# Deformable-convolution stage: one PSUM bank for the projection, three for the transposes, rows duplicated by DMA, positions on VectorE

## What is computed

```
yp = iy + ky + offset[..., 0]          # 8 groups, 9 taps
xp = ix + kx + offset[..., 1]
val = bilinear sample of coarse_up at (yp, xp), zero outside
val = val * mask
out = einsum('bhwkc,kcf->bhwf', val, weight) + bias
x + relu(out) + fine_cal
```

## Time and profile before

| | us |
|---|---|
| median of three runs | 3746.47 |
| lowest, highest run | 3738.88, 12106.46 |
| profiled execution | 3750.21 |
| its span | 3748.5 |

### The profile page before, as it was taken

One profiled execution on the slowest core, in us unless ns is written; L12 is line 12 of the kernel. 1 busy time (PEld: TensorE's weight loads), 2 busy tenths in 40 slices (PEclk: granted clock), 3 DMA queues, 4 the chain that ended last, 5 costly groups with the idle time before them and its releaser, 6 DMA issues.

```text
span 3748.5 us, 103646 instructions
## 1 busy us (share of the span) xinstructions
PE 3383.5 (90%) x39276; PEld 3082.7 (82%) x39276; DVE 2643.4 (71%) x4029; ACT 1636.7 (44%) x3018; POOL 1300.2 (35%) x1358
## 2 busy tenths in 40 slices
PE   8979999999999947998888998998899898988998
PEld 7869999999999936888787887887788787877888
DVE  3446666666666548878876887886887887688882
ACT  0021211211221215656654665664666665566663
POOL 1000000000000025645645555554654655455451
PEclk9989999999999978999998999998999998999998
DMA  4232232222223221111112111112111112111110
GB/s 160 78 122 42 48 72 42 48 53 39 51 51 43 32 49 30 29 32 31 31 32 32 32 33 29 31 34 32 29 33 31 30 34 36 25 33 32 31 27 23
DMA packets 352248, 159.43 MB, mean 43 GB/s; under 512 B 228724, under 2 KB 346884, under 8 KB 351620
## 3 DMA queue, kind: packets, MB, share of 16 engines
q1 hardware_dynamic: 325456, 109.56, 17.4%
q10 hardware_dynamic: 21724, 26.37, 2.1%
q0 software_dynamic: 4608, 16.78, 1.2%
HBM read 104.60 MB, written 55.23 MB: 43 GB/s over the span
## 4 chain that ended last, share of the span: by engine, by line
PE 44%; issue 7%; ACT 6%; DVE 2%; POOL 2%; ACTq 1%; DMA 1%; SPq 1%; POOLq 0%; DVEq 0%
PE eb L1420 25%; PE tb L981 9%; PE vb L1003 9%; ACT wtT L986 4%; ACT ot L1025 1%; ACT res L1012 1%; DVE wt L975 1%; PE tb L911 1%; DMA win<-cpad 1%; ACTq L1316 1%; PE vb L1018 1%; ACT val L1289 1%; ACTq L882 0%; DVE val L1362 0%; SPq L1083 0%
## 5 line engine op out<-in xcount | busy, mean ns | idle before, releaser
L1420 PE MATMUL eb<-val,wd 128*128 128x256 f32 (+2 forms) x8172 | 1269.5, 300 | 9.5 <-POOL gate L1212 8.5
L1420 PEld LDWEIGHTS eb<-val,wd 128*128 128x128 f32 x8172 | 1080.6, 199 | 44.8 <-issue 35.4
L975 DVE TENSOR_TENSOR wt<-taps_all 128x576 f32<-128x576 f32 x1024 | 938.6, 984 | 52.5 <-PE tb L981 44.6
L981 PE MATMUL tb<-ident,wt 128*128 128x128 f32 x4608 | 715.9, 282 | 63.8 <-ACT wtT L986 45.3
L986 ACT COPY wtT<-tb 128x512 f32<-128x512 f32 x1152 | 651.8, 593 | 164.8 <-PE tb L981 126.0
L1362 DVE TENSOR_TENSOR val<-vb,val 128x432 fp32r<-128x432 f32 (+1 forms) x768 | 382.6, 552 | 411.0 <-ACT val L1289 409.2
L981 PEld LDWEIGHTS tb<-ident,wt 128*128 128x128 f32 x4608 | 504.7, 141 | 185.5 <-ACT wtT L986 103.6
L1289 ACT CAST val<-vb 128x432 fp32r<-128x432 f32 (+1 forms) x768 | 342.1, 524 | 706.4 <-PE vb L1003 706.2
L480 PE MATMUL conv<-fine,wf 128*108 128x256 f32 x4608 | 591.1, 289 | 7.6 <-DVE omT L751 7.6
L480 PEld LDWEIGHTS conv<-fine,wf 128*108 128x108 f32 x4608 | 570.5, 173 | 23.0 <-issue 23.0
L1003 PE MATMUL vb<-wtT,win 64*32 64x144 f32 x16384 | 350.2, 309 | 184.3 <-issue 93.3
(11 more groups left out here) (138 smaller groups left out, 3175.7 us busy)
## 6 DMA issues: line engine op xcount, KB each, us to landing
win<-cpad SPq DMA_DIRECT2D x304, 64.0 KB
om_s<-om_d SPq DMA_DIRECT2D x1152, 12.0 KB
chunk<-in_x SPq DMA_DIRECT2D x32, 512.0 KB, 5.9
xchunk<-in_x SPq DMA_DIRECT2D x32, 512.0 KB, 4.2
r_d<-r POOLq DMA_DIRECT2D x32, 512.0 KB, 3.2
rt<-r_d SPq DMA_DIRECT2D x63, 256.0 KB, 2.9
out<-ot ACTq DMA_DIRECT2D x63, 256.0 KB, 2.2
om_d<-omT SPq DMA_DIRECT2D x64, 216.0 KB
```

The costliest lines, as they stand in the source:

```text
L975: return nc.vector.tensor_tensor(wt[:, g * NK:(g + 1) * NK, WQ * u:WQ * (u + 1)].rearrange("p k (a b) -> p k a b", a=WIN), of_group(0).uns ...
L981: last = nc.tensor.transpose(tb[b][:, 128 * j:128 * j + 128], wt[:, 4 * i + j, :], ident[:])
L1420: done = nc.tensor.matmul(eb[fo][:, W * r0:W * r1], wd[wp][:, half, k, 128 * fo:128 * fo + 128], source[:, at:at + r1 - r0, cols], start=f ...
```

## The change

- `eb` becomes two halves of one PSUM bank; the freed bank makes `tb` three banks, bank i % 3 for batch i. Batch i then waits for the copy of batch i-3.
- LATE = KEPT = 18, FIRST = 3: in every half slot PE now transposes batches 0 to 2 right after the second sampling run, then projects 18 products of dy 2, then does the third sampling run, then batches 3 to 8 with no projection between them.
- `val` gets a tenth row, so that every strip's tap rows lie one after another: the split into 128-column pieces goes, and every strip has 72 instructions before sampling. The rows that the split avoided are duplicated by four DMAs on SP's queue before every second strip (`duplicate_rows`); POOL waits for them one strip later. The POOL copies at L1190 go, and the crossing has two steps instead of three.
- The nine instructions of positions and coefficient move from POOL to the end of DVE's slot (s, 1) (`locate`).
- ACT's tap activations for the right half move from the end of slot (s, 0) to the end of slot (s, 1).
- Tables for row positions hold 16 strips instead of 64. The path for large offsets is changed to match and does not run.

The core of the diff:

```diff
-        VROWS, VCOLS = 9, W + 2
+        VROWS, VCOLS = 10, W + 2
-        tb = [bank(f"tb{i}") for i in range(2)]
+        tb = [bank(f"tb{i}") for i in range(3)]
-        eb = [bank(f"eb{i}") for i in range(2)]
+        eb_all = bank("eb")
+        eb = [eb_all[:, 256 * fo:256 * fo + 256] for fo in range(CH)]
...
-            LATE, KEPT = 8, 8
+            DUPLICATES = 2 * CH
+            LATE, KEPT, FIRST = 18, 18, 3
...
+                def duplicate_rows(s):
+
+                    done, read = (4 * s, s - 1) if isinstance(s, int) else (sp.to_reg(4 * s), sp.to_reg(s - 1))
+                    sp.wait_ge(consts, CONSTS)
+                    w(sp, "sides", done)
+                    w(sp, "old_read", read)
+                    for v in val:
+                        for half in range(CH):
+                            sp.dma_start(v[:, half, 0:6, 0:2].bitcast(f32), v[:, half, 0:6, 8:10].bitcast(f32)).then_inc(sems["duplicated"], 16)
...
                     elif known(s - 1, 0, ST):
+                        if turn is None or turn % 2 == 0:
+                            duplicate_rows(s)
                         w(sp, "summed", s - 1)
...
-                    if p == 1 and known(s, 0, ST):
+                    above, under = slice(0, 3), slice(6, 9)
+                    if p == 0 and (not isinstance(s, int) or 2 <= s <= ST):
+                        h(pool, "duplicated", 8 * DUPLICATES * s)
+                    if crossing is not None:
                         for v in val:
-                            g.tensor_copy(v[:, :, 3:6, 0], v[:, :, 3:6, 8].bitcast(f32)).then_inc(sems["below"], 1)
...
                         side(s, p, 0)
-                        place(s + 2)
-                        weigh(s + 2, p)
                         measure(s + 2, p, 0)
...
                         taps(s + 1, 1 - p, 0)
+                    else:
                         taps(s + 1, 1 - p, 1)
...
+                def locate(s, p):
+                    if known(s, 0, ST):
+                        h(dve, "dist_ready", 4 * s)
+                        h(dve, "masked", s + 1)
+                        positions(dve, nc.vector, s, sems["pchain"], NPOS * s)
+                        h(dve, "pchain", NPOS * (s + 1))
+                        nc.vector.tensor_tensor(coef[p][:], lo[:, 0], mask[:], ALU.mult).then_inc(sems["coef_ready"], 1)
...
                     else:
                         for g in range(3):
                             product(s + 1, 1 - p, 0, g)
+                        locate(s + 2, p)
...
-                        pieces = ((0, 2, 7), (2, 4, 1)) if dy == 0 and q == 0 else ((0, 4, dy - 1 if q == 0 else 3 + dy),)
-                        if rows == W:
-                            pieces = [(0, 1, (7, 0, 1)[dy])]
+                        at = dy + 4 * q
...
                     for i in range(NT):
+                        if i == FIRST:
+                            if owed:
+                                last = project(target, q, rest[0:LATE])
+                                if u == 0 and LATE >= len(rest):
+                                    last.then_inc(sems["projected"], 1)
+                            if sampling:
+                                h(pe, "val_lo", 6 * (n - 1) + 2)
+                                sample_blocks(2, window).then_inc(sems["sampled"], 1)
                         if known(s, 0, ST):
                             w(pe, "products", 8 * n + 2 * ((4 * i + 3) // NK + 1))
-                            w(pe, "tb_out", batch_no(s, u, i) - 1)
-                            transpose_batch(i, bank_no(s, p, u, i)).then_inc(sems["batched"], 1)
+                            w(pe, "tb_out", batch_no(s, u, i) - (0 if u and i == 0 else 2))
+                            transpose_batch(i, bank_no(i)).then_inc(sems["batched"], 1)
```

More of the change, by code:

```diff
@@ L1288, in half_slot @@
                                 at, m = 1 + 32 * hx + 12 * v, bank_of(h, v).shape[3]
[L1289 removed]
+                                nc.scalar.copy(val[0][:, h, :, 2 + 4 * q:6 + 4 * q, at:at + m], bank_of(h, v)
                                                ).then_inc(sems["val_hi"], 1)
@@ L1385, in dve_fast @@
                 bx = base_x[:].rearrange("p s (u v) -> p s v u", u=3)
-                for table, n, end, done in ((by, ST, H - 1, 8), (bx, 2, W - 1, 12)):
+                for table, n, end, done in ((by, SI, H - 1, 8), (bx, 2, W - 1, 12)):
                     own = table[:, :, 1, 0]
                     wide = lambda t: t.unsqueeze(2).broadcast_to([128, n, 3])
-                    at_end, at_start = edge[:, 0:n, 0], edge[:, 0:n, 1]
+                    at_end, at_start = (tap[1][:, 0, 0:n, end] for end in range(2))
                     dve.wait_ge(based, done)
@@ L1395, in dve_fast @@
                     nc.vector.tensor_tensor(table[:, :, 2], table[:, :, 1], wide(at_start), ALU.subtract).then_inc(based, 1)
+                dve.wait_ge(based, BASED)
+                for s in range(2):
+                    locate(s, s)
                 cap(0, 0, 0)
@@ L1414, in project @@
                         first = dy == 0 and half == 0 and dx == 0 and part == 0
-                        last = dy == 2 and half == CH - 1 and dx == 2 and part == 2
-                        pieces = ((0, 2, 7), (2, 4, 1)) if dy == 0 and q == 0 else ((0, 4, dy - 1 if q == 0 else 3 + dy),)
-                        if rows == W:
-                            pieces = [(0, 1, (7, 0, 1)[dy])]
-                        for piece, (r0, r1, at) in enumerate(pieces):
-                            done = nc.tensor.matmul(eb[fo][:, W * r0:W * r1], wd[wp][:, half, k, 128 * fo:128 * fo + 128],
-                                                    source[:, at:at + r1 - r0, cols], start=first and piece == 0, stop=last)
+                        last = dy == 2 and half == CH - 1 and dx == 2 and part == 2 and fo == CH - 1
+                        at = dy + 4 * q
+                        done = nc.tensor.matmul(eb[fo][:, 0:rows], wd[wp][:, half, k, 128 * fo:128 * fo + 128],
+                                                source[:, at:at + rows // W, cols], start=first and fo == 0, stop=last)
                     return done
@@ L1467, in half_slot @@
+                            transpose_batch(i, bank_no(i)).then_inc(sems["batched"], 1)
+                        if i >= FIRST and owed and LATE < len(rest):
+                            left, steps, m = rest[LATE:], NT - FIRST, i - FIRST
+                            last = project(target, q, left[len(left) * m // steps:len(left) * (m + 1) // steps])
+                            if u == 0 and i == NT - 1:
                                 last.then_inc(sems["projected"], 1)
@@ L1495, in general @@
             parts = [val_all[q][:, 0:CH * NSUM].rearrange("p (h m) -> p h m", h=CH) for q in range(2)]
-            sums = [taps_all[:, 2:4].rearrange("p q t g a -> p (q t g a)"), win_all[:, 128:128 + NSUM]]
+            spare = [tap[q].rearrange("p t g a -> p (t g a)") for q in range(1, 4)] + [win_all[:, 128:128 + NSUM // 2]]
+            sums = [[spare[2 * half + hx].rearrange("p (k y x) -> p k y x", k=NK, y=4) for hx in range(2)] for half in range(CH)]
             def w(e, name, v):
@@ L1551, in dve_general @@
                     w(dve, "coef_ready", s + 1)
-                    for half in range(CH):
-                        nc.vector.memset(sums[half], 0.0).then_inc(sems["zeroed"], 1)
+                    for tile in spare:
+                        nc.vector.memset(tile, 0.0).then_inc(sems["zeroed"], 1)
                     with dve.Fori(0, NWIN) as wy:
```

133 lines of the change are left out of this document (50 added, 83 removed).

## The result

The changed kernel takes 3808.6 us (median of 4 executions, 3806.1 to 3816.7), the kernel before beside it 3743.3: a ratio of 1.018, 95% interval 1.016 to 1.021. The profiled execution has a span of 3804.4 us where before had 3748.5.

What follows compares the result with a forecast made beforehand. PE's list was taken to set the pace, its gaps coming from ACT's copies. Turns +74, crossings -15 and +4, opening -5 sum to +58 on the profiled 3750.2, which stands 3.7 above the median: 3805 us, range 3715 to 3880.

Steps and rivals of the forecast that it cites:

- Third run and ACT's first copy: After a slot's sampling start S: third sampling run at S+5.8, 2.9 us later than before; first batch copy S+7.3, before S+4.4.
- The shorter block: PE's even-strip tap products: 72 instructions in 8.91 us instead of 108 in 12.58, gaining 3.67 us per two strips, 117 in all.
- Slots (s, 1): Half slot inside the loop: ACT's last copies end at S+13.8, so the next slot starts after 14.0 us instead of 12.06.
- To the block, plain: Slot (s, 0) without a return ahead: tap products start 12.1 us after sampling starts, before 10.66.
- clock rival: PE's clock falls before the product block in ordinary strips: one in three blocks, +170 us, 3975; chance 0.06.
- To the block, behind the return: Slot (s, 0) after PE's loop return: tap products start after 12.5 us, 12.1 plus DVE's 0.4; before 11.03.
- The slot ahead of the return: Slot ending in PE's loop return: 14.8 us, before 13.68, bounds 14.0 and 15.4; PE's restart was trusted least.
- Crossings: Three places where POOL's gate holds PE: gate about 1 us instead of 2.31, half the clock loss gone, -15; later window load +4.
- Positions on DVE: Nine position and coefficient instructions on DVE: 3.2 us, just hidden with 0.4 us of cover; 0.4 per turn at DVE's loop return.
- DVE late: Rival: DVE comes late behind its loop return, 2 us per turn instead of 0.4, +46, about 3850 us; chance 0.17.
- copies keep pace: Faster rival: ACT's nine copies end as before, near 3620 or 3710 us; needs first batch copy before S+5.5; chance 0.10.
- Change without effect: Rival: PE's list is shorter and the tail no longer than the loop's return anyway, +1 us per turn, 3760; chance 0.17.

Runs made afterwards that it cites:

- 270 waits: The changed kernel with 270 always-met waits for the constants ahead of PE's loop, nothing else differing: 3732.4 us, ratio 0.997 to the kernel before.
- 130 waits: The changed kernel with 130 always-met waits for the constants ahead of PE's loop, nothing else differing: 3842.9 us, ratio 1.027 to the kernel before.
- the old order: Changed kernel with 8 products, then the third sampling run, then batches with other products between: 3682.5 us; with positions also back on POOL, 3575.1.

## Why the prediction was right or wrong

The time was right, 3805 against 3808.6. The mechanism, a late third run that holds ACT's copies back by more than the block saves, was right in kind. That the number was hit so closely is luck: terms were wrong in both directions, and the largest one, the place of the code, was not in the forecast at all.

- *Third run and ACT's first copy.* Forecast S+5.8 and S+7.3. Measured 5.3 and 6.7 in slots (s, 1); in plain slots (s, 0) 5.7 to 6.9 for the third run, because of clock and DVE. The three batches were priced at 0.56 each from the weight loads of the earlier trace rows; the run of 12 transposes that starts at 2677.14 is followed by the products 1.28 us later. The lateness is the cause of the loss: with the batches kept behind the third run (3670) the time falls by 138 us, and the waits at `tb` fall from 176 to 31 (1500 to 3500 us).
- *The shorter block.* 8.9 forecast, 8.96 measured, and 3.7 us per turn where no return follows.
- *Slots (s, 1).* Forecast 14.0, measured 13.1. Of the 0.9 the early first copy is 0.6. The rest is in "ACT's seventh copy starts at S+10.8": seven copies ran 0.54 apart from S+6.7 (2682.22, 3.78 for seven), so the seventh started near S+9.9, 3.2 behind the first and not 3.5. I had queued PE's six batches and the result's transposes one after another behind the first copy, but three banks let PE work beside ACT.
- *To the block, plain.* Forecast 12.1. In the slot shown, 11.9 (2688.61 to 2700.55); in the turn without a return 11.5 and 11.8. The median is 12.9: in 16 of 26 such slots the first run, behind its 2.35 us wait for ACT, takes 2.2 to 3.1 us instead of 1.7, at a lower clock (0.69 from 2761 to 2764 us), and in 9 the third waits 0.4 for DVE. In the kernel before, behind waits of 1.65, none of 26 does. My clock rival named the product block, which stayed at 9.0; the loss came one step earlier, in the sampling run.
- *To the block, behind the return.* Forecast 12.5, measured 15.7, and this is the term that was most wrong: I took the return's gap over from the earlier trace rows as one gap of a given size. The second gap and the clock behind both are 2.6 us per turn, as the 270 waits show. The slot ahead of the return, the step that I trusted least, took 14.1 and not 14.8.
- *The base.* I set 71.2 against an undisturbed turn of 68.9. The median turn of before is 70.0, since it too loses clock behind its return (12.0 to the block, not 11.0). By it the forecast turn costs +1.2 and not +2.3 us. The run with 270 waits has that turn (71.4), but not its parts: in the table's order its four slots are off by -0.8, +0.8, -0.4 and +0.6.
- *Crossings.* Forecast -15 + 4, measured -34: the two strips at each of the three crossings take 54 us more than regular ones before, in sum, and 20 after. All three blocks behind the gate kept full speed (9.0 instead of 20.7), where I had halved that chance, and the gate held 1.2 instead of 2.3. The opening, forecast -5, gave nothing: the first block starts at 1454.6, before at 1454.3.
- *The sum.* From the first to the last product block, 60 strips: the median turn goes from 70.0 to 73.6, 30 turns at +3.65 are +110, the crossings -34, and the turns ahead of the first return and those that kept the clock -18, in all +58; 3666.0 - 1454.6 against 3607.9 - 1454.3 is +58.
- *Positions on DVE.* Forecast 3.2 us, measured 3.0, hidden with little cover: 4.7 us of waits in 12 turns. The rival "DVE late" fell. That they are dear under the early third run, where nothing hides them, was not in the forecast, nor needed.

The rival "copies keep pace" fell by its own mark, the first copy at S+5.5: the run that meets that mark (S+5.5, with 18 products and no batches ahead) is the one at 3670 (in its slots (s, 1)). "Change without effect" (3760) cannot be told from the place of the code: 270 waits bring the same work to 3732.

## What to carry to other kernels

Before a change of one or two per cent in a kernel with a loop is put down to its work, shift its code by some waits that are always met, in both versions: here that alone moved three kernels by 49 to 111 us. A turn ahead of the loop's first return, if the program has one, compares the work alone. A queue that must do A before B (ACT's values before its copies) is served by bringing A forward, not by giving the feeding engine more of B first. Work that is free on an engine at one order can cost 107 us at another, so move it and the order in separate runs.

## What the runs showed of the hardware

- Entering the loop cost PE nothing. At a return it stood 3.1 to 3.7 us ahead of the first sampling run in the two kernels compared, up to 4.8 with 130 waits, and 2.2 to 2.8 in the versions with the old order and no waits, where a plain slot waits 1.9 for ACT. Nine of the fourteen programs also break off 29 to 61 matmuls later, for 0.2 to 2.2 us. The break moved by 32 pairs of instructions when 65 were added ahead of the loop. Behind both the granted clock was 0.50 for 3 us, 0.66 on average over the next 5, then 1.00.
- DVE's products took 0.69 us each alone (six in 4.15) and 1.70 beside POOL's distances (two in 3.40, with POOL at L950 from 2689.72 to 2692.55). The Trainium skill, "SBUF — State Buffer", section "Who interferes with whom", says that a DVE instruction with two inputs in SBUF contends with one of GpSimd that reads SBUF; the trace agrees. The 0.98 each that I had taken from the earlier trace rows is a mean over all states.
